# A four-layer graph network: edge messages from outer products of destination groups, sorts rearranged, the gated update transposed

## The reference

```
L0: x += segment_sum(x[src] * edge_weight, dst) @ W
L1: h = relu(bn(cat(x[src], x[dst]) @ W1 + b1)); h = relu(bn(h @ W2 + b2)); x += segment_sum(h, src)
L2: two graph convolutions: segment_sum(h[src] * norm, dst) + h * inv_deg + b
L3: eh = relu(edge_attr @ en1.T + b); w_e = (eh @ en2.T + b).reshape(-1, 32, 32)
    six times: m = relu(segment_sum(einsum('ei,eio->eo', out[src], w_e), dst) + conv_bias)
               out = gru(m, out)
```

## Time and profile before

| | us |
|---|---|
| median of 3 runs | 42,712.97 (42,701.56 to 42,723.61) |
| profiled execution, its own time | 42,514.04 |
| its span, first to last instruction | 42,512.1 |
| TensorE busy, share of the span | 71% |
| VectorE busy | 68% |
| ScalarE busy | 27% |
| GpSimd busy | 73% |
| mean granted TensorE clock | 0.794 of 2.4 GHz |

### The profile page before, as it was taken

How to read it: one execution, slowest core, us unless ns; L and a number is a source line. 1 busy time by engine, 2 the same in 40 slices (tenths; PEclk the granted TensorE clock), 3 DMA queues, 4 the chain that set the end, 5 groups by cost and what they waited for, 6 DMA issues and landing times. The chain is left out here.

```text
span 42512.1 us, 515826 instructions
## 1 busy us (share of the span) xinstructions
PE 30160.5 (71%) x99425; PEld 18121.0 (43%) x99426; DVE 29047.4 (68%) x63440; ACT 11318.4 (27%) x26426; POOL 30972.7 (73%) x31499
## 2 busy tenths in 40 slices
PE   5222234444465222249999999999999999999999
PEld 5332323333365222234444444444444444444444
DVE  7333322221155222249999999999999999999999
ACT  0000001111110000014444444444444444444444
POOL 1666655555503665669998999899899989998997
PEclk8555556655555555569999999999999999999999
DMA  1110012210031010011111111111111111111111
GB/s 45 41 41 24 20 35 62 62 34 21 21 76 23 12 12 12 12 25 46 46 45 44 46 45 45 45 46 45 44 46 45 46 44 46 45 46 44 45 46 42
DMA packets 1365766, 1669.90 MB, mean 39 GB/s; under 512 B 847196, under 2 KB 1012047, under 8 KB 1252303
## 3 DMA queue, kind: packets, MB, share of 16 engines
q1 hardware_dynamic: 664232, 1115.69, 8.2%
q0 software_dynamic: 669696, 495.09, 7.3%
q10 hardware_dynamic: 31680, 57.69, 0.4%
HBM read 1393.98 MB, written 274.47 MB: 39 GB/s over the span
## 5 line engine op out<-in xcount | busy, mean ns | idle before, releaser
L1706 PE MATMUL l3m_p_w<-en,l3m_hid 128*128 128x512 f32 x42240 | 20965.3, 619 | 656.8 <-DVE l3m_prod L1772 398.8
L1756 DVE TENSOR_REDUCE l3m_xg<-l3m_prod 128x32 f32<-128x1024 f32 x10560 | 12858.1, 1218 | 168.6 <-POOL l3m_prod L1637 0.8
L1628 POOL DMA_INDIRECT l3m_xg<-wide_table,l3m_mt x10560 | 10341.0, 979 | 2395.8 <-issue 2033.1
L1637 POOL TENSOR_TENSOR l3m_prod<-l3m_rest,l3m_xg 128x384 f32<-128x384 f32 x10560 | 10673.0, 1011 | 281.9 <-ACT l3m_rest L1683 93.7
L1706 PEld LDWEIGHTS l3m_p_w<-en,l3m_hid 128*128 128x128 f32 x42240 | 7164.5, 189 | 6865.7 <-issue 5224.6
L1683 ACT COPY l3m_rest<-l3m_p_w 128x384 f32<-128x384 f32 x10560 | 5050.6, 478 | 12815.6 <-PE l3m_p_w L1706 12187.2
L1768 DVE TENSOR_TENSOR l3m_prod<-l3m_p_w,l3m_xg 128x512 f32<-128x512 f32 x10560 | 7196.1, 681 | 429.2 <-PE l3m_p_w L1706 257.4
L1718 PEld LDWEIGHTS l3m_p_sum<-l3m_xg,l3m_apart 128*125 128x125 f32 x21120 | 3965.2, 188 | 5090.7 <-issue 2742.2
L1671 ACT ACTIVATE l3m_apart<-iota_lo,l3m_mt 128x125 f32<-128x125 f32 x10560 | 4238.6, 402 | 0.5 <-DMA l3m_mt<-dst_meta 0.5
L1718 PE MATMUL l3m_p_sum<-l3m_xg,l3m_apart 128*125 128x64 f32 x21120 | 3473.9, 246 | 23.0 <-DVE l3m_xg L1756 23.0
L858 POOL DMA_INDIRECT l2a_xg<-table,l2a_mt x1760 | 1676.7, 953 | 2443.5 <-DMA l2a_mt<-dst_meta 1896.8
(11 more groups left out here) (328 smaller groups left out, 22546.9 us busy)
## 6 DMA issues: line engine op xcount, KB each, us to landing
l3m_hid<-hid_t SPq DMA_DIRECT2D x660, 1024.0 KB
l3m_xg<-wide_table,l3m_mt POOLq DMA_INDIRECT x10560
hid_t<-l_hid SPq DMA_DIRECT2D x110, 1024.0 KB, 4.1
order_src_bk<-dst_bucket SPq DMA_DIRECT2D x52, 808.0 KB
order_dst_bk<-src_bucket SPq DMA_DIRECT2D x52, 808.0 KB
by_dst<-order_src_empty SPq DMA_DIRECT2D x28, 1071.0 KB, 24.4
l_rec<-by_dst SPq DMA_DIRECT2D x110, 272.0 KB
l_xg<-table,l_mt POOLq DMA_INDIRECT x1760
```

The lines of the kernel that those rows point to most:

```text
L1628: pool.indirect_dma_start(xg[s][:, j, 0:2 * D], None, wide_table[:, :], bass.IndirectOffsetOnAxis(ap=mt[s][:, j, 0:1].bitcast(I32), axis=0 ...
L1637: pool.tensor_tensor(o_i(prod[j % RING][:, OWN:HD]), o_i(rest[j % RING][:, :]), state_of(s, j, REST), ALU.mult).then_inc(pooled, 1)
L1706: ins = pe.matmul(p_w[j % 2][:, c * 512:(c + 1) * 512], hid[s][:, j * P:(j + 1) * P], en2[:, c * 512:(c + 1) * 512], start=True, stop=True)
L1756: dve.tensor_reduce(xg[s][:, j, 2 * D:3 * D], o_i(prod[j % RING][:, :]), AX, ALU.add).then_inc(msgs, 1)
```

## The change

**Sorts.** In keys, only source buckets are counted now, with one comparison and four matmuls of 400 columns a round. The sort into `by_src` runs first. Its target and `by_dst` are both filled in it, the latter by ScalarE's queue (44 DMAs). Destination degrees are counted in it too: two more VectorE comparisons and 32 bfloat16 matmuls a chunk. The sort into `by_dst` is a new function, `order_groups`: it orders edges by (lo, group of 8 buckets), and each such group begins at a multiple of 32 edges. Per chunk it has a broadcast of 4,096 keys to 128 partitions, 32 comparisons (`match`), a per-group counter in PSUM that 16 ScalarE copies bring back to TensorE, and 32 sends. There is no fill in it.

**Tiles.** A tile of `by_dst` is now four strips of 32 edges, each strip within one group of 8 buckets. With the padding this takes NQ = 2,064 tiles (86 blocks of 24, each block 4 sets of 6), in place of 1,760.

**l0**: the edge network works on 24 of the new tiles in each of the first 86 groups, and stores `eh` with edges on partitions. **l2a, l2b** become `dst_sum`: sets of 6 gathers, one matmul of 32 columns a tile, and partial sums of 96 strips per block, joined by a triangular matrix `sub_seg` and stored; at the end 13 gathers bring each group's last sum to ACC. No additions at register offsets remain. The joining matrices are made by **GpSimd in l1b** (172 operations of 96 columns and 11 of up to 768). **l1b** also makes its mask one group earlier, and in **l1c** the loads wait for `hits` and no more for `summed`.

**l3m**: per strip TensorE makes an outer product over the strip's 32 edges, [128 hidden] x [32 inputs x 8 slots]; ScalarE copies three quarters of it to SBUF and VectorE one quarter; then TensorE multiplies by `en2_i` over the 128 hidden for each of the 32 inputs, in four column strips. VectorE's only other work per tile is `spread` (256 columns). The message itself is never made. GpSimd only gathers. **The update** moves into the same block, with features on partitions: biases come with the activations, and a quarter takes seven matmul calls and two transposes, of which one each are for the next table.

The core of the new l3m (constants: SET = 6, SETS = 4, QB = 24, TWOS = 3, SUB = 32, SLOTS = 8, PAIRS = 192, PW = 256, MIX_AT = ((0, 1, 2), (3, 4, 5), (6, 7))):

```diff
-                            for c in range(2):
-                                ins = pe.matmul(p_w[j % 2][:, c * 512:(c + 1) * 512], hid[s][:, j * P:(j + 1) * P],
-                                                en2[:, c * 512:(c + 1) * 512], start=True, stop=True)
+                        def times(b, k, j):
+                            t = k * TWOS + j
+                            pe.wait_ge(spreads, b * QB + (2 * t + 2 + SPREADS))
...
+                            for q in range(2):
+                                for x in range(2):
...
+                                    for c in range(2):
+                                        rows = slice((2 * x + c) * SUB, (2 * x + c + 1) * SUB)
+                                        ins = pe.matmul(half(t, x)[:, c, :, q * SLOTS:(q + 1) * SLOTS],
+                                                        eh[k][rows, 2 * j + q, :], spread[(2 * t + q) % RING][rows, :, :],
+                                                        start=True, stop=True)
...
+                        def mix(k, n):
+                            for c in range(4):
+                                ins = pe.matmul(p_pair[c * D:(c + 1) * D, 0:PAIRS], en2_i[:, 4 * n + c, :],
+                                                outer[k % 2][:, 4 * n + c, :], start=n == 0, stop=n == D // 4 - 1,
+                                                skip_group_check=True)
...
+                        def bias(k):
+                            for j in range(SET):
+                                c = j % 4
+                                to = p_pair[c * D:(c + 1) * D, 0:PAIRS].rearrange("p (c q s) -> p q c s", c=4, s=SLOTS)
+                                ins = pe.matmul(to[:, j], xg[k][:, j, D:2 * D], mt[k][:, j, 1:MW],
+                                                start=False, stop=False, skip_group_check=True)
...
+                            act.wait_ge(outers, b * (2 * TB) + (2 * t + 1 + OUTERS))
+                            act.copy(outer_of(k, j)[:, 0], half(t, 0)[:, 0]).then_inc(act_moved, 1)
+                            act.wait_ge(outers, b * (2 * TB) + (2 * t + 2 + OUTERS))
+                            act.copy(outer_of(k, j)[:, 2:4], half(t, 1)).then_inc(act_moved, 1)
...
+                            for q in range(2):
+                                at = (2 * t + q) * SLOTS
+                                dve.tensor_tensor(spread[(2 * t + q) % RING][:, :, :],
+                                                  xg[k][:, 2 * j + q, 0:D][:, :, None].broadcast_to([P, D, SLOTS]),
+                                                  p_hit[:, at:at + SLOTS][:, None, :].broadcast_to([P, D, SLOTS]),
+                                                  ALU.mult).then_inc(spreads, 1)
...
+                                    pool.wait_ge(spreads, b * QB + (k * SET + j + 1))
+                                    pool.sem_inc(begun, 1)
+                                    pool.indirect_dma_start(
+                                        xg[k][:, j, :], None, wide_table[:, :],
+                                        bass.IndirectOffsetOnAxis(ap=mt[k][:, j, 0:1].bitcast(I32), axis=0)).then_inc(rows_in[k], 16)
```

What the first sort gains per chunk, and TensorE's part of the second:

```diff
+                                dve.wait_ge(tallied, c + 1)
+                                for to, of, n in ((one_lo, d_lo, LO), (one_b, d_b, NB)):
+                                    ins = dve.tensor_tensor(to[:, :, :], p_iota[:, None, 0:n].broadcast_to([P, CC, n]),
+                                                            of[s][:, :, None].broadcast_to([P, CC, n]), ALU.is_equal)
+                                ins.then_inc(ends_hit, 1)
...
+                            for t in range(CC):
+                                ins = pe.matmul(p_deg[0:LO, 0:NB], one_lo[:, t, :], one_b[:, t, :],
+                                                start=False, stop=True, skip_group_check=True)
...
+                            for m in range(PAIRS):
...
+                                pe.wait_ge(copied, n + 1)
+                                pe.matmul(to[:, j, :], at_row[:, j, :], now[m % 2][0:K, :],
+                                          start=True, stop=False, skip_group_check=True)
+                                for t in range(2):
+                                    ins = pe.matmul(p_now[0:K, 0:D0], lo_one[s][:, j + t, :], d_one[s][:, j + t, :],
+                                                    start=False, stop=True, skip_group_check=True)
+                                ins.then_inc(counted, 1)
```

More of the change, by code:

```diff
@@ L45 @@
 EPS = 1e-5
-PLACE = 32
 W = NB * D
@@ new lines, in mixes, with block_of @@
+                        def mixes(k, j):
+                            if j == TWOS - 1:
+                                bias(k)
+                            for n in MIX_AT[j]:
+                                ins = mix(k, n)
+                            if j == TWOS - 1:
+                                ins.then_inc(mixed, 1)
+                        def block_of(b, first=False):
+                            for k in range(SETS):
+                                for j in range(TWOS):
+                                    times(b, k, j)
+                                    if first and k == 0:
+                                        continue
+                                    if j == 0:
+                                        mix_begin(b, k)
+                                    mixes((k - 1) % SETS, j)
+                                    if k == 2 and j == TWOS - 1 and not first:
+                                        pe.wait_ge(taken, b * SETS + (1 + TAKEN))
+                                        sums.join(pe, b)
@@ L1850, in _ @@
+                        sums.start_act(act)
+                        act.sem_inc(act_moved, ACT_MOVED)
+                        act.sem_inc(taken, TAKEN)
+                        block_of(0, first=True)
+                        with act.Fori(1, NBLK) as b:
+                            block_of(b)
+                        take(NBLK, 0)
+                        take(NBLK, 1)
+                        sums.take_total(act, act.copy, NBLK)
+                        sums.store(act, NBLK)
                         for n in range(Q + 3):
```

1435 lines of the change are left out of this document (997 added, 438 removed).

## The result

| | the result's runs | e15 |
|---|---|---|
| before, median | 42,718 us (4 runs) | 39,851 us (7 runs) |
| after, median | 51,542 us (4 runs) | 33,826 us (4 runs) |
| ratio, 95% interval | **1.2068** (1.2043 to 1.2093) | **0.8486** (0.8472 to 0.8500) |

What follows compares the result with a forecast made beforehand. It took l3m's six steps (23,670 of 42,512 us) as decisive, no engine alone bounding them. Steps -5,470, keys -420, sorts and l0 up, l1 and l2 down: -5,640, giving 36,870, with 0.47% 37,040; range 34,700 to 41,500.

Steps and rivals of the forecast that it cites:

- TensorE's term: Messages of l3m: TensorE needs 8.5 us a set, 2,924 us a step, above GpSimd's floor; chance 0.40 for 8 to 9.5.
- TensorE runs out of instructions: Second sort: slow single TensorE records might return with 288 instructions a chunk; bound +1,000 us, +50 taken.
- Weight loads taking turns at 0.11: TensorE in l3m: strips overlap but weight loads follow each other at 0.11 us, giving 8.7 us a set.
- pairs no shorter than 0.09: Rival for l3m: no weight load and matmul pair under 0.09 us; 9.5 to 11.9 us a set, 39,000 to 44,000; chance 0.13.
- the in-order rival: Rival for l3m: TensorE's passes start in order, 12.2 us a set, 45,000 in all; chance 0.19 together with a slow clock.
- The floor of GpSimd: Messages of l3m: six gathers of 1.25 us make 7.5 us a set, 2,580 us a step.
- The rival that I gave 0.27: GpSimd's gathers bound l3m's messages, strips and weight loads running side by side; 34,800 us in all; chance 0.27.
- The copies: Copies out of PSUM in l3m: ScalarE 1.05 us for 1,024 columns, 0.59 for 512; VectorE 0.65 for 512.
- Around a step: From a step's last message to the next step, update included: 110 us, against 106 before.
- The sorts: First sort +300 us and +50 for filling `by_dst` under the sends; second sort +50, its bounds -300 and +1,000.
- l1c: Phase l1c: loads start a matmul group earlier, ending VectorE's 204 us wait, TensorE being next; -140 us.
- l2: Phases l2a and l2b: 2,064 gathers of 1.25 us and 40 us for join and 13 gathers; -70 us for both.

Runs made afterwards that it cites:

- e15: The changed kernel as it is, in rounds with the kernel before: 33,826 us beside 39,851, ratio 0.8486.
- held chip: Kind of chip or occasion, met in two experiment runs: kernel before 42,734 us, changed kernel 51,544; the result's own runs are like it.
- free chips: Kind of chip or occasion, met in the other sixteen experiment runs, on four chips: kernel before 39,851 to 39,921 us.
- e10: The changed kernel as it is, on a free chip: 33,798 us beside 39,864 for the kernel before.
- e17: The changed kernel with each gather of the steps' messages replaced by a plain load on SyncE's queue: 32,615 us.
- The bench: Separate kernel of short stretches, TensorE running 2,560 passes beside one load at a time, only on free chips: 81 us beside gathers, 83 alone.

## Why the prediction was wrong

**The step that failed** is TensorE's term, 8.5 us a set, and with it the overlap that the sum took for granted, that TensorE's records run beside GpSimd's gathers. On the held chip a set took (5,225 - 194) / 344 = 14.6, gathers and TensorE's work one after the other. Six steps came out 7,636 us longer where 5,470 less were forecast; that is 13.1 of the 14.5 ms of the miss, and l2 (+1,119 for -70) is 1.2 more. It did not fail by the array: the strips run side by side there too when records come (22 `mix` records in 1.31 us). It failed because I priced a record by its distance in a phase whose GpSimd multiplies between gathers, and put it into a phase whose GpSimd only gathers. Why records come slowly there on a held chip and not on a free one stays open. The warning was in my own rows. The earlier trace rows have the single records 2 us apart, and I kept "TensorE runs out of instructions" for the second sort, at up to 1,000 us. l2b took 1.51 us a gather where gathers alone need 1.25, and I read this as room that the change would use. On free chips l2a takes 1.29 a gather with either kernel, so the 0.22 was the holding, and after pays it as well (3,239 / 2,064 = 1.57). With 127 matmul records a set, if only one in ten had come 2 us after the last, as there, a set would have been over 20 us, far above the 11.2 that I gave as the point where the change loses (an estimate).

**By part**, with the free column, where the mechanisms can be read:

*The strips.* Timeline of TensorE in e10 (one set's end and the next pairs of tiles):

```profile
20005.82 1.15 PE L2379 MATMUL l3m_p_outer<-l3m_spread,l3m_eh 32*128 32x256 f32 x16
20006.90 1.18 PE L2394 MATMUL l3m_p_pair<-l3m_outer,en_i 128*32 128x192 f32 x24
20008.01 1.15 PE L2379 MATMUL l3m_p_outer<-l3m_spread,l3m_eh 32*128 32x256 f32 x16
20009.08 1.18 PE L2394 MATMUL l3m_p_pair<-l3m_outer,en_i 128*32 128x192 f32 x24
20010.19 1.15 PE L2379 MATMUL l3m_p_outer<-l3m_spread,l3m_eh 32*128 32x256 f32 x16
```

A pass of `times` costs 1.15 / 16 = 0.07 and one of `mix` 1.18 / 24 = 0.05, against the 0.21 and 0.16 that I had estimated for passes alone, about three times less each. Weight loads taking turns at 0.11 and pairs no shorter than 0.09 are both refuted, the in-order rival too: it wanted 0.2 between `times` records. Six changes between kinds cost nothing that shows (2.18 us from one pair of tiles to the next, 1.15 + 1.18 being its work). The Trainium skill, "TensorE: Matmul & The Clock Gate", Part 3, gives 3.07 times for four row strips; 0.21 / 0.072 = 2.9 is near it, with 0.21 an estimate from passes of 512 columns.

- *The floor of GpSimd*, 7.5 us, was exact: 29.97 us a block on free chips, gathers 1.249 apart. The rival that I gave 0.27 is what happens there; my 8.5 was a microsecond too dear. Over the whole step it is 7.8 a set, because eight of the last nine blocks take 38 to 47 us. There q0, the queue of the gathers, fills 63.9% of the DMA engines' time with 5,930 packets in 330 us (18800 to 19130 of e10), where the 330 us from 18000 have 14.5% with 8,467. The tiles of these blocks are, by an estimate, padding alone (212,500 edges and 15.5 empty places on the mean in each of 1,625 groups fill 77 of the 86 blocks), and `by_dst` is filled with one and the same source index (N) for such tiles, so all of their gathers read one row. That this makes the packets long no run tests; it costs some 110 us a step. With plain loads in place of the gathers (e17) the last blocks take 29.1 like the others.
- *The copies* were right: 1.02 us for 1,024 columns (1.05 estimated), 0.59 for 512 on ScalarE, 0.69 on VectorE (0.65), `spread` 0.41.
- *Around a step*: 193 us from the last gather of a set to the next step's first, on both kinds of chip, where I had 110.
- *keys*: -445 for -420. *l1b*: -22 and -27 for -20.
- *The sorts*: I had +300, +50 and +50. On free chips the first grows by 6 us and the second by 18: sends cover both chains. On the held chip they grow by 40 and 351, by place in the program; there my "slow records grow with their count" is what one sees, but in the second sort, where TensorE has 144 records a chunk. That the held sum, +391, is near my +400 is luck: the terms were wrong in opposite directions. The first sort's "64 records" more are 32 matmul records and 32 weight loads (96 records a chunk for 64).
- *l1c*: -51 for -140. VectorE's wait for loads went from 204 us to 4, but 151 us of idle time that the trace puts down to issue stand at the same line (1.4 a group). *l0* with the weights: +283 held, -3 free.
- *l2*: +797 on free chips and +1,119 on the held one for -70, the one mechanism that I had wrong everywhere. 304 gathers more a phase at 1.25 are 380; l2a and l2b before stand on the same floor (2,274 = 1,760 x 1.25 and 75 for the ends).

From span to span the change is -6,116 on free chips (33,796 less 39,912); I had -5,640. As a difference the forecast was within 0.5 ms of that, and 14.5 ms off the result that it was made for. That nearness is partly luck, since the steps and the sorts came out better than I had them and l2 worse. My chance of 0.19 for slower was spent on the array's order and the clock, not on this. One slip of the sum: the gathers' rival, 34,800, stands without the 0.47% between the profiled execution and the median; with it, it is 35,000.

**What stays open.** What makes a chip held, and whether it is the chip or the occasion; whether gathers cause it or only show it; and whether the late increments make the slow records or both have one cause. The held runs I have are of the two kernels alone. The bench and the plain loads on a held chip would test the gathers, and the same chip at another time the rest.

No version beats both kernels everywhere. On free chips after itself is the best that computes the whole (33,826). On a held chip the rows suggest the kernel before with the new keys and the new waits of l1c, 446 + 50 us less; it wasn't run.

## What to carry to other kernels

A phase in which GpSimd does nothing but indirect DMAs can cost very different amounts from one chip, or one occasion, to another (5,225 and 2,879 us for a step here), and the trace of one run shows which it was: look for waits whose releaser is "remote" and long over, and for an engine's records that come singly with "issue" before them, and treat both as a price that every phase of that kind may pay. Before a change moves work into many short TensorE records beside such gathers, ask what a record costs there, not where the profile is comfortable. And measure before and after on more than one chip, and more than once on each, before believing a ratio, whatever its interval: 1.207 and 0.849 here, each good to 0.3%.

## What I had not expected of the hardware

- The same program takes 42,730 us on one chip and 39,850 to 39,920 on four others, at the same 1.249 us from gather to gather.
- On the held chip one of TensorE's increments arrived 27.7 us after its instruction's end in the block of l2a shown, and about two thirds of its increments in l2a came over 0.1 us late; in l1b and l1c, which have no gather, every one came within 0.02 us.
- The Trainium skill, "SBUF — State Buffer", Who interferes with whom, says that a DMA never contends with a compute engine. On free chips the bench agrees (81 us beside gathers, 83 alone). On the held chip TensorE has 5.5 weight loads a us with gather packets in flight and 12.0 without; whether that is contention, no run shows.
- Products of a 128x32 weight and 32 columns start 0.032 us apart at full clock, two float32 passes in 0.064.
